# A graph attention layer on one core: eight gather buffers instead of four, and all 98 table scatters behind the last gather

## The chip, the core and the metric

The kernel runs on one core of a Trainium2 chip. The metric is the device time of one execution in microseconds (us). The core has five engines that matter here: TensorE (PE), VectorE (DVE), ScalarE (ACT), GpSimd (POOL) and SyncE (SP). Each runs its own list of instructions in order, and they wait for one another through semaphores. Direct DMAs are issued by SP; indirect DMAs, which take row numbers from memory, by POOL.

## What is computed

The reference is one layer of a graph network, on 50,000 nodes with 256 features and 12,500 edges plus one self loop a node. Cut to what matters:

```python
h = relu(layernorm(x))
xs, xd = (h @ W_src.T), (h @ W_dst.T)            # 8 heads of 32
alpha = sum(xs[src] * a_s[etype]) + sum(xd[dst] * a_d[etype])   # per head, loops included
alpha = leaky_relu(alpha, 0.2)
a = exp(alpha - segment_max(alpha, dst)[dst])
a = a / segment_sum(a, dst)[dst] * edge_weight
out = segment_sum(xs[src] * a, dst) + bias
h1 = layernorm(out + h, ln1)
ff = gelu(h1 @ W1.T + b1) @ W2.T + b2
result = x + layernorm(h1 + ff, ln2)
```

## The kernel before

The edges come sorted by destination. They are cut into NCH = 98 chunks of 128, handled as NPAIR = 49 pairs of chunks. The program has three stages and a piece between the first and the second.

**Edge stage** (up to some 404 us). For each pair POOL gathers four tiles of 128 rows of x (two chunks, source and destination rows) into a buffer of `xb` with four indirect DMAs (L653). DVE takes their statistics (L377, L381, and L398 to L409 once for two pairs), ACT writes the normalised and rectified rows to `h` (L417), PE transposes them (L426), ACT and DVE split the result into a high and a low part (L435, L442), and PE projects the four tiles with 24 matmuls (L459) into `ps_x` and `ps_f` or `ps_a`. ACT copies out the scores (L807, L808, and L810 after the fourth tile), and DVE then makes the messages (L1002), which SP stores. Step j of ACT's loop takes the `h` of pair j + 3 and the scores of pair j; step j of DVE's takes the statistics of pair j + 5 and the message of pair j - 1. A buffer of `xb` is free again when the `h` of its pair is written. So the gather of pair j waits on `h_ready` for pair j - XB, here j - 4.

**Between**: PE, DVE and ACT compute the softmax over each node's edges (about 404 to 446 us).

**Sum stage** (446 to 555 us). For each pair DVE weighs the loaded messages (L1223), PE adds up the edges of each node with a matrix of ones and zeros (L1442 transposes a line of destinations, ACT makes the matrix in L838 and L841, L1453 multiplies), DVE makes the record (L1230), and SP stores it in `sums`.

**Node stage** (the rest). All nodes in 98 groups of 512: POOL gathers each node's record from `sums` (L696) and the feed-forward matmuls (L1470, L1485 to L1487) follow.

To find a node's record, POOL scatters the place of each record into one of four tables in memory (`row_of`, L663), one indirect DMA of 128 entries a chunk, 98 in all. The function is `place`. Each scatter waits for the one four before it, which wrote the same table. After all of them the tables are read back (L687) and joined by DVE (L1378), and only then can the node stage gather.

POOL's order is written out by hand. 15 of the scatters stand between the gathers, one behind every third pair (`PLACE_AT`), and 83 behind the last gather. Three times among the 83 POOL also computes the reciprocal root for the first three groups of nodes (`input_rstd`, L669 and L671), ahead of scatters number 23, 33 and 73 counted from 0 (`RSTD_AT`). Each time it waits for DVE's statistics of that group (L1009 to L1017). DVE takes those of group 0 near the end of the edge stage, of group 1 right behind it, and of group 2 at step 12 of the sum stage (`STATS2_AT`).

Of the kernel before, what the change touches and what calls it, by code (L numbers as in the profile page):

```python
# [28 lines left out]
F32 = mybir.dt.float32  # L29
# [3 lines left out]
ACT = mybir.ActivationFunctionType  # L33
# [56 lines left out]
XB = 4  # L90
# [9 lines left out]
PLACE_AT = range(4, 49, 3)  # L100
RSTD_AT = (len(PLACE_AT) + 8, len(PLACE_AT) + 18, len(PLACE_AT) + 58)
# [16 lines left out]
def build(nc, x, ends_cols, next_cols, type_cols, weight_cols, dst_line, w_src_t, w_dst_t,  # L118
# [19 lines left out]
    assert D == KC * P and NODES < NR <= NROWS and NCH % 2 == 0 and NCH < P and EP % BLOCKS == 0 and NPAIR > max(RELU2_AT, PLACE_AT[-1]) and NCH > RSTD_AT[2] and D == 2 * P and QS * KC * SQ == D  # L138
# [18 lines left out]
    with ExitStack() as ctx:  # L157
# [19 lines left out]
        zt = [sb(f"zt_{n}", [P, 2, KC, GR], F32R) for n in ("hi", "lo")]  # L177
        act_hi = sb("act_hi", [P, AB, GR], F32R)
        act_lo = sb("act_lo", [P, AB, GR], F32R)

        xb = sb("xb", [P, XB, TG, D])
# [150 lines left out]

        def wide(a, dims):

            return a.to_broadcast(dims)
# [37 lines left out]
        def front_stats(eng, f):  # L373

            wait_count(eng, x_stats, TG * f.n)
            for t in range(TG):
                eng.bn_stats(stat[:, t, :], xb[:, f.off % XB, t, :]).then_inc(stat_step, 1)  # L377
            eng.wait_ge(stat_step, TG * f.n + TG)
            eng.sem_inc(dve_gate, 1)
            for t in range(TG):  # L380
                eng.bn_aggr(mv[:, f.off % 4, t, :], stat[:, t, :]).then_inc(x_stats, 1)  # L381
# [30 lines left out]
        def front_relu(eng, f):  # L412

            eng.wait_ge(x_scaled, f.n // 2 + 1)
            wait_count(eng, xt_turned, KC * (f.n - 1))
            for t in range(TG):
                eng.activation(h[:, f.par, t, :], xb[:, f.off % XB, t, :], ACT.Relu,  # L417
                               bias=shift[:, f.off % 4, t:t + 1], scale=rstd[:, f.off % 4, t:t + 1]).then_inc(h_ready, 1)
# [178 lines left out]
        def _(pool):  # L597
# [48 lines left out]
            def gather(j):  # L646
# [3 lines left out]
                for t in range(TG):  # L650
                    wait_count(pool, h_ready, TG * (j.n - XB) + t + 1)
                    at = edge_ends[:, 2 * j.n + t % 2, 1 - t // 2:2 - t // 2]
                    pool.indirect_dma_start(xb[:, b, t, :], None, x,  # L653
# [19 lines left out]
            def pair(j):  # L673
                gather(j)
                if j.n == PLACE_AT[0]:
                    pool.wait_ge(target_ready, 1)
                    pool.wait_ge(rows_cleared, 16 * RB)
                if j.n in PLACE_AT:
                    place(Step(0, PLACE_AT.index(j.n), NCH))
            pool.wait_ge(in_order, 1)  # L680
            steps(pool, pair, 0, NPAIR, *PAIR_LOOP)
            steps(pool, place, len(PLACE_AT), NCH, NCH, NCH, RB)
# [919 lines left out]
```

## Time and profile before

| | us |
|---|---|
| median of three runs | 3073.79 |
| the three runs | 3061.24, 3073.79, 3077.57 |
| span of the profiled execution | 3075.7 |
| busy in it: PE, DVE, POOL, ACT | 2838.8, 2303.7, 2211.0, 1798.2 |
| mean granted share of TensorE's clock | 0.959 |

The profiled execution is a single one. Its span, from the first to the last instruction, is the time that the sums below are made against; the table has no other time of it. The three runs differ by 16 us among themselves. Most of the time is the node stage, where PE is the busiest engine. The change touches the first 555 us.

### The profile page before, as it was taken

The numbers are of one execution on the slowest core, as the hardware profiler recorded it, in microseconds if no ns is written. First come the engines' busy times: TensorE is split into PE (matmuls) and PEld (weight loads), VectorE is DVE, ScalarE is ACT, GpSimd is POOL, SyncE is SP. The second block draws the span as 40 slices with busy tenths as digits, with TensorE's granted clock in tenths as the row PEclk, the third lists the DMA queues.
The fourth block names the chain that finished last, engine by engine and source line by source line (L and its number), as shares of the span: only waits on it lengthen the run. The fifth ranks groups of instructions, "written<-read, shape, count | busy, mean of one in ns | idle before, by whom it ended". The sixth has DMA issues, their size and how long they took to land.

```text
span 3075.7 us, 55240 instructions
## 1 busy us (share of the span) xinstructions
PE 2838.8 (92%) x18391; PEld 2581.0 (84%) x18391; DVE 2303.7 (75%) x6041; ACT 1798.2 (58%) x3180; POOL 2211.0 (72%) x1689
## 2 busy tenths in 40 slices
PE   4777747699999999999999999999999999999998
PEld 3666635589999999999999999999999999999998
DVE  5665576577777777777777777777777777777776
ACT  3555435356666666666666666666666666666664
POOL 5655555577777777777777777777777777777773
PEclk9788778899999999999999999999999999999999
DMA  6444356455555555555555555555555555555551
GB/s 150 99 112 106 89 137 212 125 129 148 145 149 149 149 147 145 144 145 144 145 149 146 144 146 147 147 144 145 144 145 145 146 146 148 147 146 146 146 138 62
DMA packets 596928, 430.65 MB, mean 140 GB/s; under 512 B 430521, under 2 KB 533471, under 8 KB 596644
## 3 DMA queue, kind: packets, MB, share of 16 engines
q1 hardware_dynamic: 563908, 348.13, 38.8%
q0 software_dynamic: 31616, 77.93, 13.7%
q8 instruction: 148, 2.42, 0.3%
q14 instruction: 136, 1.11, 0.1%
q10 hardware_dynamic: 1120, 1.05, 0.1%
HBM read 247.76 MB, written 179.26 MB: 139 GB/s over the span
## 4 chain that ended last, share of the span: by engine, by line
PE 80%; POOL 1%; DMA 0%; DVE 0%; ACT 0%; issue 0%; SPq 0%; DVEq 0%; POOLq 0%; ACTq 0%
PE ps_f L1470 35%; PE ps_x L1509 9%; PE ps_t L1485 6%; PE ps_t L1487 6%; PE ps_a L1485 6%; PE ps_a L1487 6%; PE ps_t L1486 6%; PE ps_a L1486 6%; POOL arena L696 0%; ACT arena L867 0%; DMA arena<-z_rows 0%; POOL arena L714 0%; DMA z_rows<-arena 0%; DMA arena<-sums,node_rows 0%; POOL zt_lo L734 0%
## 5 line engine op out<-in xcount | busy, mean ns | idle before, releaser
L847 ACT ACTIVATE act_hi<-ps_f,hidden_bias 128x512 fp32r<-128x512 f32 x784 | 538.2, 686 | 923.8 <-PE ps_f L1470 923.3
L1330 DVE TENSOR_TENSOR act_lo<-ps_f,act_hi 128x512 fp32r<-128x512 f32 x784 | 539.9, 689 | 468.5 <-ACT ps_f L848 401.7
L1470 PE MATMUL ps_f<-zt_hi,ffn_hi 128*128 128x512 f32 x1568 | 618.8, 395 | 7.2 <-DVE act_lo L1330 5.6
L1470 PE MATMUL ps_f<-zt_hi,ffn_lo 128*128 128x512 f32 x1568 | 620.2, 396 | 0.0
L1470 PE MATMUL ps_f<-zt_lo,ffn_hi 128*128 128x512 f32 x1568 | 618.0, 394 | 0.0
L848 ACT ACTIVATE ps_f<-ps_f,hidden_bias 128x512 f32<-128x512 f32 x784 | 511.0, 652 | 0.0
L696 POOL DMA_INDIRECT arena<-sums,node_rows x391 | 404.5, 1034 | 111.9 <-issue 92.6
L1485 PE MATMUL ps_a<-ffn_hi,act_hi 128*128 128x256 f32 x1568 | 439.8, 280 | 0.0
L1487 PE MATMUL ps_a<-ffn_hi,act_lo 128*128 128x256 f32 x1568 | 439.1, 280 | 0.0
L1485 PE MATMUL ps_t<-ffn_hi,act_hi 128*128 128x256 f32 x1560 | 438.1, 281 | 0.0
L1486 PE MATMUL ps_a<-ffn_lo,act_hi 128*128 128x256 f32 x1568 | 437.9, 279 | 0.0
L1487 PE MATMUL ps_t<-ffn_hi,act_lo 128*128 128x256 f32 x1560 | 437.4, 280 | 0.0
L1486 PE MATMUL ps_t<-ffn_lo,act_hi 128*128 128x256 f32 x1560 | 436.2, 280 | 0.0
L1470 PEld LDWEIGHTS ps_f<-zt_hi,ffn_lo 128*128 128x128 f32 x1568 | 293.9, 187 | 71.6
L1470 PEld LDWEIGHTS ps_f<-zt_hi,ffn_hi 128*128 128x128 f32 x1568 | 294.5, 188 | 44.4 <-DVE act_lo L1330 6.2
L1470 PEld LDWEIGHTS ps_f<-zt_lo,ffn_hi 128*128 128x128 f32 x1568 | 294.6, 188 | 36.1
L1485 PEld LDWEIGHTS ps_a<-ffn_hi,act_hi 128*128 128x128 f32 x1568 | 294.1, 188 | 18.1
L1486 PEld LDWEIGHTS ps_a<-ffn_lo,act_hi 128*128 128x128 f32 x1568 | 293.8, 187 | 18.4
L1486 PEld LDWEIGHTS ps_t<-ffn_lo,act_hi 128*128 128x128 f32 x1560 | 293.1, 188 | 18.2
L1485 PEld LDWEIGHTS ps_t<-ffn_hi,act_hi 128*128 128x128 f32 x1560 | 293.0, 188 | 18.1 <-issue 0.2
L1487 PEld LDWEIGHTS ps_a<-ffn_hi,act_lo 128*128 128x128 f32 x1568 | 295.2, 188 | 0.0
L1487 PEld LDWEIGHTS ps_t<-ffn_hi,act_lo 128*128 128x128 f32 x1560 | 294.2, 189 | 0.0
(243 smaller groups left out, 6665.2 us busy)
## 6 DMA issues: line engine op xcount, KB each, us to landing
xb<-in_x SPq DMA_DIRECT2D x97, 512.0 KB, 5.0
z_rows<-arena SPq DMA_DIRECT2D x97, 512.0 KB
arena<-z_rows SPq DMA_DIRECT2D x388, 128.0 KB
out<-arena SPq DMA_DIRECT2D x97, 512.0 KB, 4.3
h_rows<-h SPq DMA_DIRECT2D x96, 512.0 KB
arena<-h_rows SPq DMA_DIRECT2D x384, 128.0 KB
msgs<-arena SPq DMA_DIRECT2D x49, 256.0 KB
arena<-msgs SPq DMA_DIRECT2D x49, 256.0 KB, 6.9
```

The lines of the kernel that those rows point to most:

```text
L696: pool.indirect_dma_start(rec[:, g.par, t, :], None, sums, bass.IndirectOffsetOnAxis(ap=at, axis=0)).then_inc(rec_in[g.par], 16)
L847: act.activation(act_hi[:, m % AB, :], ps_f[:, m % 2, :], ACT.Gelu, bias=hidden_bias[:, m:m + 1]).then_inc(act_hi_ready, 1)
L848: act.activation(ps_f[:, m % 2, :], ps_f[:, m % 2, :], ACT.Gelu, bias=hidden_bias[:, m:m + 1]).then_inc(act_f_ready, 1)
L1330: dve.tensor_tensor(act_lo[:, m % AB, :], ps_f[:, m % 2, :], act_hi[:, m % AB, :].bitcast(F32), ALU.subtract).then_inc(act_lo_ready, 1)
L1470: ins = pe.matmul(ps_f[:, m % 2, 0:cols], ffn1[a][:, k, m * P:(m + 1) * P], zt[b][:, i.par, k, 0:cols], start=(j == 0), stop=(j == 3 * KC ...
L1485: pe.matmul(to, act_hi[:, m % AB, cols], ffn2[0][:, m, :], start=(m == 0 and t % 2 == 0), stop=False, skip_group_check=True)
L1486: pe.matmul(to, act_hi[:, m % AB, cols], ffn2[1][:, m, :], start=False, stop=False, skip_group_check=True)
L1487: ins = pe.matmul(to, act_lo[:, m % AB, cols], ffn2[0][:, m, :], start=False, stop=(m == MF - 1), skip_group_check=True)
L1509: ins = pe.matmul(to, xt[b][:, k, t * P:(t + 1) * P], lift[c][:, k, :], start=(j == 0 and t % 2 == 0), stop=(j == 3 * KC - 1), skip_group_ ...
```

## The change

The gathers go round eight buffers instead of four. Buffers 0 to 3 are the tensor `xb` as before. Buffers 4 to 7, `xb_early`, lie in the memory of `act_hi` and `act_lo`, which are written first in the node stage. The gather of pair j waits for the `h` of pair j - 8. No scatter stands between the gathers any more: all 98 come behind the last one. The three `input_rstd` stand ahead of scatters 14, 26 and 78. Nothing is changed in what the other engines do or in their order; they only read other buffers.

```diff
-XB = 4
+XB = 8
+XK = 4
-PLACE_AT = range(4, 49, 3)
-RSTD_AT = (len(PLACE_AT) + 8, len(PLACE_AT) + 18, len(PLACE_AT) + 58)
+RSTD_AT = (14, 26, 78)
...
+        with nc.sbuf_tensor("xb_early", [P, XB - XK, TG, D], F32) as xb_early:
+            pass
         act_hi = sb("act_hi", [P, AB, GR], F32R)
         act_lo = sb("act_lo", [P, AB, GR], F32R)
...
-        xb = sb("xb", [P, XB, TG, D])
+        xb = sb("xb", [P, XK, TG, D])
...
+        def gather_buf(f):
+
+            b = f.off % XB
+            return xb[:, b, :, :] if b < XK else xb_early[:, b - XK, :, :]
...
-                    pool.indirect_dma_start(xb[:, b, t, :], None, x,
+                    pool.indirect_dma_start(gather_buf(j)[:, t, :], None, x,
...
             def pair(j):
                 gather(j)
-                if j.n == PLACE_AT[0]:
-                    pool.wait_ge(target_ready, 1)
-                    pool.wait_ge(rows_cleared, 16 * RB)
-                if j.n in PLACE_AT:
-                    place(Step(0, PLACE_AT.index(j.n), NCH))
             pool.wait_ge(in_order, 1)
             steps(pool, pair, 0, NPAIR, *PAIR_LOOP)
-            steps(pool, place, len(PLACE_AT), NCH, NCH, NCH, RB)
+            pool.wait_ge(target_ready, 1)
+            pool.wait_ge(rows_cleared, 16 * RB)
+            steps(pool, place, 0, NCH, NCH, NCH, RB)
```

POOL's instructions at the start of the edge stage, before. L653 is a gather, L663 a scatter.

```order
L643 MEMSET arena 128x1
L653 DMA xb<-in_x,arena 128x256 x20
L663 DMA row_of<-arena 50304x1
L653 DMA xb<-in_x,arena 128x256 x12
L663 DMA row_of<-arena 50304x1
```

The same place in the changed kernel, where L661 is the gather.

```order
L651 MEMSET arena 128x1
L661 DMA xb<-in_x,arena 128x256 x16
L661 DMA xb_early<-in_x,arena 128x256 x16
L661 DMA xb<-in_x,arena 128x256 x16
L661 DMA xb_early<-in_x,arena 128x256 x16
```

The scatters behind pair 4 and every third pair after it are gone from here, and every other four pairs go to `xb_early`.

POOL from the last gathers to the reading back of the tables, before. L669 and L671 are `input_rstd`, L687 reads the tables.

```order
L653 DMA xb<-in_x,arena 128x256 x8
L663 DMA row_of<-arena 50304x1 x8
L669 TENSOR_TENSOR n_rstd<-n_var,minus_half 128x4
L671 TENSOR_TENSOR n_shift<-n_mm,n_rstd 128x4
L663 DMA row_of<-arena 50304x1 x10
L669 TENSOR_TENSOR n_rstd<-n_var,minus_half 128x4
L671 TENSOR_TENSOR n_shift<-n_mm,n_rstd 128x4
L663 DMA row_of<-arena 50304x1 x40
L669 TENSOR_TENSOR n_rstd<-n_var,minus_half 128x4
L671 TENSOR_TENSOR n_shift<-n_mm,n_rstd 128x4
L663 DMA row_of<-arena 50304x1 x25
L687 DMA node_rows<-row_of 128x391
```

The same in the changed kernel, where the lines are L661, L671, L677, L679 and L692.

```order
L661 DMA xb<-in_x,arena 128x256 x4
L671 DMA row_of<-arena 50304x1 x14
L677 TENSOR_TENSOR n_rstd<-n_var,minus_half 128x4
L679 TENSOR_TENSOR n_shift<-n_mm,n_rstd 128x4
L671 DMA row_of<-arena 50304x1 x12
L677 TENSOR_TENSOR n_rstd<-n_var,minus_half 128x4
L679 TENSOR_TENSOR n_shift<-n_mm,n_rstd 128x4
L671 DMA row_of<-arena 50304x1 x52
L677 TENSOR_TENSOR n_rstd<-n_var,minus_half 128x4
L679 TENSOR_TENSOR n_shift<-n_mm,n_rstd 128x4
L671 DMA row_of<-arena 50304x1 x20
L692 DMA node_rows<-row_of 128x391
```

Runs of 8, 10, 40 and 25 scatters have become runs of 14, 12, 52 and 20.

## Rows read from the trace of the kernel before

**Rows 1.** The page: its first line.

```profile
span 3075.7 us, 55240 instructions
```

**Rows 2.** Busy us by stage: length, PE, PEld, DVE, ACT, POOL, clock, DMA share, GB/s.

```profile
60.00:360.00 300.00, 222.20 (x1290) 205.31 (x1290) 191.53 (x678) 163.16 (x393) 173.84 (x177) 0.80 0.44 108
360.00:404.00 44.00, 31.70 (x211) 29.71 (x211) 24.96 (x87) 20.57 (x52) 11.33 (x13) 0.81 0.30 95
...
446.00:555.00 109.00, 75.78 (x331) 57.77 (x330) 69.52 (x114) 58.79 (x155) 55.86 (x56) 0.85 0.63 191
555.00:3076.00 2521.00, 2483.67 (x16420) 2264.88 (x16420) 1953.73 (x4972) 1530.25 (x2535) 1907.35 (x1365) 0.99 0.54 142
```

**Rows 3.** The gathers' line: ns min/median/max, first and last start, then idle before them.

```profile
L653 POOL DMA_INDIRECT xb<-in_x,arena x196: 943/949/5408, 9.8 to 359.3; - x196
...
  ACT h L417: 95.8, 56
  issue: 43.1, 139
```

**Rows 4.** The scatters, in the view of the tables.

```profile
L663 POOL DMA_INDIRECT row_of<-arena x98: 956/965/1992, 35.4 to 536.7; - x98
```

**Rows 5.** DVE's longest wait from 60 to 355 us: total, times, longest.

```profile
DVE arena L1002 <- ACT arena L810: 89.3, 20, 6.7
```

**Rows 6.** Timeline of the edge stage: start, us, engine, line, operation, [idle before <-releaser].

```profile
287.83 0.94 POOL L653 DMA_INDIRECT xb<-in_x,arena  x1 [0.30 <-issue]
...
290.56 0.19 ACT L810 COPY arena<-ps_a 128x32 f32<-128x32 f32 x1 [5.04 <-PE ps_f L459]
...
298.04 1.40 DVE L377 BATCH_NORM_STATS2 stat<-xb 128x6 f32<-128x256 f32 x4
...
300.94 0.29 PE L459 MATMUL ps_a<-proj_hi,zt_lo 128*128 128x272 f32 x1
...
302.54 1.01 POOL L663 DMA_INDIRECT row_of<-arena  x1 [0.31 <-issue]
...
305.42 0.19 ACT L810 COPY arena<-ps_a 128x32 f32<-128x32 f32 x1 [5.07 <-remote]
...
307.37 0.97 POOL L653 DMA_INDIRECT xb<-in_x,arena  x1 [3.82 <-ACT h L417]
...
318.87 0.19 ACT L810 COPY arena<-ps_a 128x32 f32<-128x32 f32 x1 [3.67 <-PE ps_x L459]
```

**Rows 7.** Timeline: POOL's first long pause, before the gather of pair 6.

```profile
47.66 0.95 POOL L653 DMA_INDIRECT xb<-in_x,arena  x1 [6.20 <-ACT h L417]
```

**Rows 8.** Timeline of ACT and POOL at the end of the edge stage.

```profile
354.60 2.10 ACT L417 ACTIVATE h<-xb,shift,rstd 128x256 f32<-128x256 f32 x4
...
371.16 0.97 POOL L663 DMA_INDIRECT row_of<-arena  x1 [1.25 <-DMA row_of<-arena]
...
373.75 2.08 ACT L417 ACTIVATE h<-xb,shift,rstd 128x256 f32<-128x256 f32 x4
...
399.58 1.06 POOL L669 TENSOR_TENSOR n_rstd<-n_var,minus_half 128x4 f32<-128x4 f32 x1 [27.45 <-DVE n_mm L1017]
...
401.95 0.19 ACT L810 COPY arena<-ps_f 128x32 f32<-128x32 f32 x1 [0.79 <-PE ps_f L459]
```

**Rows 9.** Timeline of the sum stage, all engines.

```profile
449.26 0.69 DVE L1230 TENSOR_TENSOR arena<-ps_a,rows 128x512 f32<-128x512 f32 x1 [1.63 <-PE ps_a L1453]
...
465.60 1.03 PE L1453 MATMUL ps_a<-arena 128*128 128x256 f32 x4
...
477.62 0.96 POOL L663 DMA_INDIRECT row_of<-arena  x1 [0.30 <-issue]
...
478.90 0.69 DVE L1230 TENSOR_TENSOR arena<-ps_a,rows 128x512 f32<-128x512 f32 x1 [13.79 <-remote]
...
495.96 1.41 POOL L669 TENSOR_TENSOR n_rstd<-n_var,minus_half 128x4 f32<-128x4 f32 x1 [17.38 <-DVE n_mm L1017]
...
554.05 0.69 DVE L1230 TENSOR_TENSOR arena<-ps_a,rows 128x512 f32<-128x512 f32 x1 [0.17 <-PE ps_a L1453]
```

More of the change, by code:

```diff
@@ L137, in build @@
     NQ = GR // SQ
-    assert D == KC * P and NODES < NR <= NROWS and NCH % 2 == 0 and NCH < P and EP % BLOCKS == 0 and NPAIR > max(RELU2_AT, PLACE_AT[-1]) and NCH > RSTD_AT[2] and D == 2 * P and QS * KC * SQ == D
+    assert NB == XK and (XB - XK) * TG * D == 2 * AB * GR and (NPAIR - NB) % XB > XK and NPAIR % XB == 1
+    assert D == KC * P and NODES < NR <= NROWS and NCH % 2 == 0 and NCH < P and EP % BLOCKS == 0 and NPAIR > RELU2_AT and NCH > RSTD_AT[2] and D == 2 * P and QS * KC * SQ == D
     sums = nc.dram_tensor("sums", (EP + P, D), F32, kind="Internal").ap()
@@ L376, in front_stats @@
             for t in range(TG):
-                eng.bn_stats(stat[:, t, :], xb[:, f.off % XB, t, :]).then_inc(stat_step, 1)
+                eng.bn_stats(stat[:, t, :], gather_buf(f)[:, t, :]).then_inc(stat_step, 1)
             eng.wait_ge(stat_step, TG * f.n + TG)
@@ L416, in front_relu @@
             for t in range(TG):
-                eng.activation(h[:, f.par, t, :], xb[:, f.off % XB, t, :], ACT.Relu,
+                eng.activation(h[:, f.par, t, :], gather_buf(f)[:, t, :], ACT.Relu,
                                bias=shift[:, f.off % 4, t:t + 1], scale=rstd[:, f.off % 4, t:t + 1]).then_inc(h_ready, 1)
```

## The prediction

> **What bounds the kernel now.** I read the busy times by stage first, then the waits inside each stage. The node stage is 2521 us of the 3075.7, with PE busy 98.5% of it [rows 1, 2]. The change touches nothing there, so the sum concerns the first 555 us: how early the node stage can begin. It begins when two things are done, DVE's last record at 554.05 + 0.69 us [rows 9] and the scatters with the reading back of their tables. The last scatter starts at 536.7 [rows 4]. That is 17 us before DVE is through, and the landing and the reading back lie between, so DVE's records end last, but the scatters have no more than those few microseconds to spare.
>
> In the edge stage no engine is full: from 60 to 360 us PE is busy 74%, DVE 64%, POOL 58%, at a granted clock of 0.80 [rows 2], between the levels of 1.2 and 2.4 GHz. POOL sits idle 95.8 us until ACT has written an `h` [rows 3]. That looks like a shortage of buffers. But the reader should see in [rows 6] when the data of one pair is wanted. The last gather of pair 38 is issued by 288.77, and DVE comes to its statistics at 298.04, straight from its earlier work, with no idle time before them. The data is not what DVE waits for. DVE waits for ACT's L810 before L1002, 89.3 us in 20 waits [rows 5], and L810 waits for PE.
>
> That last wait is the odd one. The last matmul of pair 33 starts at 300.94 and takes 0.29 us, yet ACT's copy of its result starts at 305.42, after 5.07 us of idleness [rows 6]. So PE's signal comes about 4.2 us after its matmul. What happens at 305.42? POOL's run of indirect DMAs ended at 303.55. The same is seen at 290.56, where the run had ended at 288.77: 1.8 us after the run in both. Then `h` is written, POOL starts its next two gathers of four DMAs, and the cycle begins again. The sum stage shows the same thing more clearly: PE's L1453 starts at 465.60 and DVE's record of it at 478.90, after 13.79 us idle, 0.3 us after POOL's last scatter of a long run ended at 478.58 [rows 9]. I take as the working rule that PE's increments arrive late while POOL issues indirect DMAs back to back, and arrive when POOL pauses. Why that is so, no row tells.
>
> **The scatters taken out of the edge stage.** The cycle of two pairs that holds a scatter lasts 305.42 - 290.56 = 14.86 us, the next one, without, 318.87 - 305.42 = 13.45 [rows 6]. A scatter lengthens POOL's run and with it the cycle by 1.4 us. Thirteen of the 15 stand before the gather of pair 44: 13 x 1.4 = 18 us gained by the time that the `h` of pair 40 is written. That one stands two cycles before the 354.60 of pair 44 [rows 8], at 354.6 - 14.9 - 14.9 = about 325.
>
> **Four more buffers, in the steady state.** POOL issues a gather as soon as an `h` frees a buffer, with four buffers and with eight. It is always the faster one: a gather takes 0.95 + 0.31 us [rows 3], a pair 5.0 us against cycles of 6.7 us a pair. The cycle stays at 13.45 and I cost this part at nothing. What hides the gathers is the 9 us by which they lead; it becomes some 36 us.
>
> **Four more buffers, at the start.** Before, POOL issues six pairs and then pauses 6.2 us until 47.66 [rows 7]. Now ten pairs are free to go: four pairs x 5.0 = 20 us more of unbroken run, to about 60 us. If PE's increments wait for its end, the start loses 60 + 2 - 45 = 17 us. If they leak through as fast as in the cycles, it loses nothing. No row shows so long a run of gathers; I take the middle, 9 us, and keep 0 and 18.
>
> **The end of the edge stage.** The `h` of pair 40 is then written at 325 - 18 + 9 = 316, and the last gather, pair 48's, is issued by 322, where before it ended at 360.3. Now come 14 scatters instead of 8. The eight took from 360.3 to 372.1 [rows 3, 8], 1.5 us each, and in that time the edge stage stood almost still: no `h` between 354.60 and 373.75 [rows 8]. Fourteen take 21 us, to 343, and I expect the `h` of pair 42 at 345. Behind it ACT has ten steps. From 373.75 to 401.95 it made seven, 4.0 us each [rows 8], with POOL quiet. Five of the ten carry DVE's statistics as well, which add 1.2 us: 5 x 5.2 + 5 x 4.0 = 46. The stage ends at 391 instead of 402, **11 us earlier**, 2 to 20 by the bounds of the start.
>
> **The sum stage.** POOL then has 12 + 52 scatters to the third `input_rstd`, where it had 10 + 40. The 50 took from 399.58 to 478.58 [rows 8, 9]. The 14 more cost 1.27 us each, 18 us, so POOL gets there at 478.6 - 11 + 18 = 486. Against that stands DVE: it must reach step 12. Before, it made five records from 449.26 up to POOL's pause at 478.9, 5.9 us each, and the remaining six in the 17 us behind, 2.8 us each [rows 9]. Now its first record is at 438 and 48 us go by until the pause: eight records, and four steps are left, 11 us. The third `input_rstd` is then at 497, against 495.96. The wait there shrinks from 17.4 us to 11.
> Behind it stood 25 scatters, about 1.6 us each to 536.7 [rows 4, 9]; now 20, over by 530. The records that follow step 12 took from 496 to 554.7 and keep their pace; five fewer scatters beside them may give 1.5 us. So the sum is +1 - 1.5, and the likely end of DVE's records lies between 552 and 556. The gain of the edge stage is given back, since the scatters cost about the same beside the sum stage.
>
> **The sum.** 3075.7 - 11 (edge stage) + 12 (longer way from there to step 12) - 1.5 (fewer scatters behind it) gives 3075. POOL's idle time before the first `input_rstd`, 27.45 us [rows 8], grows to about 45, and PE runs freely in it; for what the 5.2 us a pair may be too high there I take off 2 us, an estimate without a row: 3073. The bounds of the start, 9 us either way, shift it all. The median of the runs stood 1.9 us below the span, so the prediction is **3071 us**, 3061 to 3081 for this likeliest case.
>
> **Rival A: the buffers were the bound.** The Trainium skill, Perfetto Trace Analysis, section Optimization Strategy, says that the same gap repeating on an engine that should be saturated can mean too few buffers. POOL's 3.8 us before every other pair [rows 6] is such a gap. As a mechanism of this kernel: POOL would run on at 5.0 us a pair and the rest follow at the 5.2 us a pair used above. From pair 2's `h`, at about 47 [rows 7], 47 more pairs take 245 us, so that the edge stage ends near 300 and some 90 to 100 us go: 2975 to 2985, or about 3025 if half of it comes. Against it stands the 9 us that a pair's data lies unused. I give 0.08. By that rule the kernel gains 3%; by [rows 6] nothing comes of the buffers.
>
> **Rival B: slower.** PE's increments stay away for as long as POOL does not pause. The start then loses 18 us, the run of 52 scatters lets DVE make six records only, and six steps at 2.8 us are left at the pause: the third `input_rstd` comes at 478.6 - 2 + 18 + 17 = 512, and the records end at 512 + 59 = 571, 16 us late: **3090**. It decides from the point at which fewer than seven records stand before the pause. For it speaks the 13.79 us wait [rows 9], against it that five records did get through earlier. The same section of the skill's Perfetto Trace Analysis advises to interleave stages with different busiest engines, which this change undoes; that would come out on this side. I give 0.15 to slower by over 0.5%.
>
> **Rival C: faster by more.** The start loses nothing, so that the edge stage ends 20 us earlier, and DVE makes its records at 4 us each beside the scatters, so that it is at step 12 when POOL gets there, at 478.6 - 20 + 18 = 477 instead of 496. The records then end some 19 us earlier: 3050 to 3058. I give 0.19.
>
> **How the numbers follow.** The likeliest case has 0.58, A 0.08, B 0.15, C 0.19. A difference under 0.5%, 15 us, is about what a measurement cannot tell from none. Faster by over that is A and most of C, with a little of the likeliest's edge: 0.26; slower is B: 0.14; the same 0.60. The range leaves out A and the far ends of B: 3042 to 3090.
>
> **What the profile would show.** No scatter row before the last gather, which ends near 322 (315 to 332); POOL's first long pause at 60 or later; 13.4 to 13.5 us from one long wait of L810 to the next; POOL idle 40 us or more before the first `input_rstd`, at about 389; the third near 497, after a wait shorter than 17 us; the last record at 550 to 558. Wrong it would be if the cycle gets clearly shorter than 13.45 us, if DVE is seen waiting for a gather, if PE's signals come in time during POOL's long runs, or if the node stage, 2521 us, changes in length.

## The result, and the profile after

The changed kernel takes 3077.12 us, the kernel before 3061.64, medians of 20 executions each, taken side by side (3064.95 to 3087.50 without one execution of 3602.31 at a granted clock of 0.742, and 3051.36 to 3077.57). The ratio is 1.0044, 95% interval 1.0029 to 1.0059. So the change costs 0.44%, 13.5 us, where I forecast about 3 us less than the 3073.79 that stood for the kernel before. The new time lies inside my range; the direction is wrong.

One thing comes first. The profile that the prediction was read from has a span of 3075.7 us [rows 1], and its execution took 3077.57: of the 20 executions of that kernel it is the slowest. The profile after is from an execution of 3070.53 us, one of the shorter ones. Held against each other these two say that the change gains 7 us. A later profile of the kernel before (run e16) has a span of 3057.7, from an execution of 3059.41 us, near the 3061.64 of this comparison, and is the better partner. But it comes from a chip on which the kernel before takes 3075 us in the median, and it was the fastest of its ten there. Both profiles are used below, and a second one of the changed kernel (e15, 3076.17 us) beside them.

The page of the kernel after, its first line, and then the busy time by stage (length, PE, PEld, DVE, ACT, POOL, clock, DMA share, GB/s), which answers to [rows 2]:

```profile
span 3068.8 us, 55240 instructions
```

```profile
60.00:360.00 300.00, 216.28 (x1376) 204.04 (x1375) 198.25 (x703) 169.58 (x409) 167.42 (x171) 0.86 0.35 107
...
446.00:555.00 109.00, 68.86 (x306) 51.49 (x306) 67.15 (x111) 53.27 (x142) 57.25 (x57) 0.86 0.67 197
555.00:3068.00 2513.00, 2482.76 (x16418) 2266.62 (x16418) 1952.94 (x4967) 1531.81 (x2535) 1908.91 (x1365) 0.99 0.54 142
```

PE's busy time in the node stage is 2482.76 us against 2483.67 in [rows 2]. As forecast, all that happens lies ahead of it. The timeline of the kernel after shows the places (start, us, engine, line, operation, then the idle time and its releaser). First the start and the end of the edge stage:

```profile
57.38 2.08 ACT L425 ACTIVATE h<-xb,shift,rstd 128x256 f32<-128x256 f32 x4 [2.91 <-remote]
72.58 2.08 ACT L425 ACTIVATE h<-xb,shift,rstd 128x256 f32<-128x256 f32 x4
...
73.45 0.95 POOL L661 DMA_INDIRECT xb<-in_x,arena  x1 [7.94 <-ACT h L425]
...
329.80 1.02 POOL L671 DMA_INDIRECT row_of<-arena  x1 [0.30 <-issue]
...
345.77 0.97 POOL L671 DMA_INDIRECT row_of<-arena  x1 [3.44 <-DMA row_of<-arena]
...
383.53 1.06 POOL L677 TENSOR_TENSOR n_rstd<-n_var,minus_half 128x4 f32<-128x4 f32 x1 [25.44 <-DVE n_mm L1022]
...
385.90 0.19 ACT L815 COPY arena<-ps_f 128x32 f32<-128x32 f32 x1 [0.79 <-PE ps_f L467]
```

POOL's first pause comes at 73.45 instead of 47.66 [rows 7], and the edge stage ends at 385.90 instead of 401.95 [rows 8]. Then the way to the first record and the sum stage:

```profile
411.55 2.08 ACT L827 ACTIVATE h<-xb,n_shift,n_rstd 128x256 f32<-128x256 f32 x4 [19.32 <-POOL n_shift L679]
...
441.65 0.69 DVE L1235 TENSOR_TENSOR arena<-ps_a,rows 128x512 f32<-128x512 f32 x1 [1.63 <-PE ps_a L1458]
...
497.18 1.04 POOL L677 TENSOR_TENSOR n_rstd<-n_var,minus_half 128x4 f32<-128x4 f32 x1
...
498.53 2.08 ACT L827 ACTIVATE h<-xb,n_shift,n_rstd 128x256 f32<-128x256 f32 x4 [11.55 <-POOL n_shift L679]
...
503.83 0.69 DVE L1235 TENSOR_TENSOR arena<-ps_a,rows 128x512 f32<-128x512 f32 x1 [12.97 <-PE ps_a L1458]
...
546.06 0.69 DVE L1235 TENSOR_TENSOR arena<-ps_a,rows 128x512 f32<-128x512 f32 x1 [0.50 <-PE ps_a L1458]
```

The same places in the better profile of the kernel before, e16:

```profile
54.78 2.08 ACT L417 ACTIVATE h<-xb,shift,rstd 128x256 f32<-128x256 f32 x4
...
398.58 1.06 POOL L669 TENSOR_TENSOR n_rstd<-n_var,minus_half 128x4 f32<-128x4 f32 x1 [18.17 <-DVE n_mm L1017]
400.95 0.19 ACT L810 COPY arena<-ps_f 128x32 f32<-128x32 f32 x1 [0.79 <-PE ps_f L459]
...
417.68 2.07 ACT L822 ACTIVATE h<-xb,n_shift,n_rstd 128x256 f32<-128x256 f32 x4 [10.80 <-POOL n_shift L671]
...
448.28 0.69 DVE L1230 TENSOR_TENSOR arena<-ps_a,rows 128x512 f32<-128x512 f32 x1 [1.63 <-PE ps_a L1453]
...
484.21 1.33 POOL L669 TENSOR_TENSOR n_rstd<-n_var,minus_half 128x4 f32<-128x4 f32 x1
...
495.21 2.06 ACT L822 ACTIVATE h<-xb,n_shift,n_rstd 128x256 f32<-128x256 f32 x4
...
536.54 0.69 DVE L1230 TENSOR_TENSOR arena<-ps_a,rows 128x512 f32<-128x512 f32 x1 [0.64 <-PE ps_a L1453]
```

Read the changed kernel's rows against those of e16. Its edge stage ends 15.1 us earlier. The first record comes only 6.6 us earlier: ACT, which makes the exp behind its second `input_relu`, waits 19.32 us for POOL's second `input_rstd` instead of 10.80. The last record comes 9.5 us later: between the first and the last lie 104.4 us instead of 88.3. And of the 16 us between these, 13 are one wait that e16 does not have. ACT comes to its third `input_relu`, in step 26 of the sum stage, and POOL has not made the third `input_rstd`; PE then waits for ACT, 12.0 us, and DVE for PE, 12.97. In e16 POOL had begun it 11 us before ACT came. The spans differ by 11.1 us, the medians by 15.5.

The profile of e15 repeats this: the edge stage ends at 387.81, ACT waits 23.36 us ahead of the exp and 14.16 for the third `input_rstd`, which POOL begins at 506.81 without a wait of its own, and DVE then waits 15.38 us; the last record starts at 552.93.

### The profile page after: what moved, and what is told of

It is laid out like the page before. It is cut to its first block, busy times and chain, and to the rows that moved or that the text cites. A ratio compares the mean times of both kernels' runs of the same rounds, so it can differ in the third digit from the quotient of the medians.

```text
span 3068.8 us, 55240 instructions
## 1 busy us (share of the span) xinstructions
PE 2815.0 (92%) x18391; PEld 2565.3 (84%) x18391; DVE 2304.9 (75%) x6041; ACT 1799.2 (59%) x3180; POOL 2211.3 (72%) x1689
## 4 chain that ended last, share of the span: by engine, by line
PE 80%; POOL 1%; DMA 0%; DVE 0%; ACT 0%; issue 0%; SPq 0%; DVEq 0%; POOLq 0%; ACTq 0%
PE ps_f L1475 35%; PE ps_x L1514 9%; PE ps_t L1492 6%; PE ps_t L1491 6%; PE ps_a L1492 6%; PE ps_t L1490 6%; PE ps_a L1491 6%; PE ps_a L1490 6%; DMA arena<-z_rows 0%; POOL arena L701 0%; ACT arena L872 0%; POOL arena L719 0%; DMA arena<-sums,node_rows 0%; DMA z_rows<-arena 0%; POOL zt_lo L739 0%
## 5 line engine op out<-in xcount | busy, mean ns | idle before, releaser
L1475 PEld LDWEIGHTS ps_f<-zt_lo,ffn_hi 128*128 128x128 f32 x1568 | 295.5, 188 | 33.5
```

Of the source, the lines that this page charges most:

```text
L1475: ins = pe.matmul(ps_f[:, m % 2, 0:cols], ffn1[a][:, k, m * P:(m + 1) * P], zt[b][:, i.par, k, 0:cols], start=(j == 0), stop=(j == 3 * KC ...
```

## The experiments

The runs fell on five chips, and they are of two kinds. On three of them the kernel before takes 2965 us (runs e1 to e12), on the two others 3062 and 3075 (e13 to e15, and e16 to e18). The comparison above is of the second kind. I call them the 2965 chips and the 3062 chips. A ratio always compares kernels on the same chip; two ratios that stand side by side can be from two chips of one kind (e1 to e4, e5 to e8 and e9 to e12 each had one chip).

**e1: the kernel before again.** No edit.

> The kernel before, unchanged, for a second profile and for what two timings of one kernel differ by. The profile that the prediction rests on has a span of 3075.7 us, the longest of 20 executions, whose median is 3061.6. Theory L (the sum started from an unlucky execution): the second profile is some 10 to 15 us shorter, and the difference lies in the sum stage and the stalls of PE and DVE there, so that its last record ends near 540 instead of 554. Theory N (the node stage differs from execution to execution): the last record ends near 554 again and the node stage is shorter than 2521 us by 10 or more. The ratio should be 1.000, within 0.002.

2964.22 against 2965.27 us, ratio 1.0000, 0.9991 to 1.0009. It told nothing of L and N, as it was another kind of chip: the edge stage ends at 308.35 instead of 401.95. The waits of e1 from 60 to 355 us (engine and line, what they waited for: total, times, longest) show why:

```profile
POOL xb L653 <- ACT h L417: 20.8, 50, 4.8
DVE stat L377 <- DMA xb<-in_x,arena: 12.2, 8, 3.3
...
DVE arena L1002 <- ACT arena L810: 7.2, 6, 2.1
```

The wait of [rows 5], 89.3 us, is 7.2 here. POOL issues just as many DMAs back to back, but PE's increments are not late. The last matmul of one tile in e1 ends at 199.68, and ACT copies its result at 199.72, in the middle of a run of POOL's:

```profile
199.39 0.29 PE L459 MATMUL ps_a<-proj_hi,zt_lo 128*128 128x272 f32 x1
...
199.72 0.20 ACT L810 COPY arena<-ps_a 128x32 f32<-128x32 f32 x1
```

POOL's idle time before a gather that an `h` releases is 0.4 us on average, hardly more than the 0.3 us before any other, so its own issuing is the pace: on the 2965 chips I read the edge stage as bound by POOL. With the scatters out of it (e3) it ends 13.1 us earlier, at 295.22, which fits.

**e2 and e8: the buffers alone.**

```diff
-RSTD_AT = (14, 26, 78)
+PLACE_AT = range(4, 49, 3)
+RSTD_AT = (len(PLACE_AT) + 8, len(PLACE_AT) + 18, len(PLACE_AT) + 58)
```

> The change's first part alone: eight gather buffers, and the 15 scatters between the gathers as before. Theory S (the start is what costs): POOL's first run has ten or more pairs, the relu of pair 3 comes near 72 instead of 50.6, the edge stage stays some 16 us behind, and the time is 3071 to 3080, ratio 1.003 to 1.006. Theory T (the scatters beside the sum stage are what costs): the start is caught up before the edge stage ends, and the time is 3058 to 3066, ratio 0.999 to 1.001.

> The kernel of e2 again, eight buffers with the scatters in their old places, beside the others. Both theories: a ratio of 0.997 to 0.999 if these executions have an edge stage of about 300 us as in e1; where the edge stage takes some 390 us, as in the two profiles shown first, the longer first run of gathers costs it up to 17 us at the start and the ratio is 1.000 to 1.005.

0.9977 (0.9968 to 0.9986) and 0.9980 (0.9971 to 0.9989): a gain, which neither theory had. The edge stage ends 2.7 us earlier in e2 than in e1, and DVE's waits for gathers fall from 12.2 us to 4.6 + 3.6, as its waits from 60 to 355 us say:

```profile
DVE stat L386 <- DMA xb<-in_x,arena: 4.6, 3, 2.1
DVE stat L386 <- DMA xb_early<-in_x,arena: 3.6, 3, 2.8
```

Where the gathers only just keep up, four more buffers seem to hide some late landings. The first gather of node records comes 2.8 us earlier than in e1, at 448.65; the spans differ by 5.4, and the rest was not followed.

**e3: the scatters alone,** with four buffers.

```diff
-PLACE_AT = range(4, 49, 3)
-RSTD_AT = (len(PLACE_AT) + 8, len(PLACE_AT) + 18, len(PLACE_AT) + 58)
+RSTD_AT = (14, 26, 78)
...
-                if j.n in PLACE_AT:
-                    place(Step(0, PLACE_AT.index(j.n), NCH))
...
-            steps(pool, place, len(PLACE_AT), NCH, NCH, NCH, RB)
+            steps(pool, place, 0, NCH, NCH, NCH, RB)
```

> The change's second part alone: four gather buffers as before, and all 98 scatters behind the last gather. Theory S: the edge stage gains the 18 us of the thirteen scatters, the longer row of scatters costs about as much behind it, and the time is 3055 to 3066, ratio 0.998 to 1.001. Theory T: the scatters beside the sum stage hold back the third input_rstd and the records by 10 to 20 us more than the edge stage gains, and the time is 3071 to 3080, ratio 1.003 to 1.006.

1.0039, 1.0025 to 1.0053, as T has it: on this kind of chip the whole loss is the scatters'.

**e4: the start held.**

```diff
-                    wait_count(pool, h_ready, TG * (j.n - XB) + t + 1)
+                    wait_count(pool, h_ready, TG * (j.n - (XK if j.n < 12 else XB)) + t + 1)
```

> The changed kernel, but the gathers of pairs 4 to 11 wait for the h of the pair four before, as with four buffers; from pair 12 on all eight are used. Theory S: the relu of pair 3 is back near 50, the burst comes later, at pairs 12 to 15, when PE is busy, and costs less than 17 us there; the time is 8 to 15 us below the changed kernel's, 3062 to 3069. Theory T: the start is of no weight, since POOL has the same scatters to make behind it; the time stays at 3074 to 3080.

1.0036, 1.0023 to 1.0050: nothing gained. e2 and e3, on the same chip, add up to 1.0016, so holding the start is if anything dearer. There is no late start to mend here: the `h` of pair 3 comes at 39.66 in e4, and at 40.27 in e5, where the first run of gathers is long. On the 2965 chips that run is of no weight, and Theory S fails.

**e5 and e15: the changed kernel again,** on either kind.

> The changed kernel, unchanged, for a second profile beside a second one of the kernel before. Both theories expect a ratio near that measured before, 1.003 to 1.006. Theory R (ACT waits for POOL's second and third input_rstd, which now stand behind 26 and 76 scatters in a row instead of 18 and 58): the profile has an ACT wait of 20 us or more for the second, ahead of the exp, and the first record comes 8 us or more later, against the end of the edge stage, than in the kernel before. Theory Q (the last scatter ends late, and the reading back with it): the reading back of the tables starts 10 us or more later than in the kernel before on the same chip, and behind DVE's last record or right beside it.

> The changed kernel a third time, for what the first comparison (1.0044) and e5 (1.0016) differ by. If the kernel before is at about 2965 us in these executions, both theories expect 1.001 to 1.003. If it is at about 3060, as in the first comparison, Theory S (the long first run of gathers delays PE's signals at the start, and the edge stage is bounded by them) expects 1.003 to 1.006 with the relu of pair 3 later by 15 us or more than in the kernel before.

e5: 1.0016, 1.0007 to 1.0025, smaller than expected, and close to the sum of the parts (-0.0023 of e2, +0.0039 of e3). e15: 1.0036, 1.0010 to 1.0061, with the relu of pair 3 at 73.06. In e5 both signs are seen, that of R in the first row, that of Q in the second. (The reading back is a direct DMA that POOL itself issues, so it stands behind all of POOL's scatters.) The rows below those are e1's:

```profile
334.09 2.07 ACT L827 ACTIVATE h<-xb,n_shift,n_rstd 128x256 f32<-128x256 f32 x4 [34.74 <-POOL n_shift L679]
...
449.94 0.60 POOL L692 DMA_DIRECT2D node_rows<-row_of  x1 [6.48 <-DMA row_of<-arena]
```

```profile
324.49 2.07 ACT L822 ACTIVATE h<-xb,n_shift,n_rstd 128x256 f32<-128x256 f32 x4 [10.21 <-POOL n_shift L671]
...
433.51 0.69 DVE L1230 TENSOR_TENSOR arena<-ps_a,rows 128x512 f32<-128x512 f32 x1 [0.50 <-PE ps_a L1453]
435.19 0.59 POOL L687 DMA_DIRECT2D node_rows<-row_of  x1 [4.71 <-DMA row_of<-arena]
```

**e6: the `input_rstd` early.**

```diff
-RSTD_AT = (14, 26, 78)
+RSTD_AT = (8, 18, 58)
```

> The changed kernel with its three input_rstd at scatters 8, 18 and 58 instead of 14, 26 and 78: as many scatters stand between the last gather and each of them as in the kernel before, and the 15 others behind the third. Theory R: ACT's wait ahead of the exp goes back to about 10 us, the records come 10 to 15 us earlier, and the ratio falls from 1.004 to 0.998 to 1.001. Theory Q: the exp and the first records come earlier as well, but the last scatter ends where it did, so the gather of the node records moves by less than 5 us; the ratio stays at 1.002 to 1.004.

1.0014, 1.0005 to 1.0023: nothing gained against e5, as Q has it. The cause that R names was there and is gone, but something else ends last. In the rows of e6 the last record is 24 us earlier than in e5, at 429.65, and the tables are read back at 450.17 as before; DVE stands idle for them, 24.86 us:

```profile
429.65 0.69 DVE L1235 TENSOR_TENSOR arena<-ps_a,rows 128x512 f32<-128x512 f32 x1 [0.51 <-PE ps_a L1458]
...
450.17 0.60 POOL L692 DMA_DIRECT2D node_rows<-row_of  x1 [4.51 <-DMA row_of<-arena]
...
455.20 1.77 DVE L1383 TENSOR_TENSOR node_rows<-node_rows,arena 128x391 int32<-128x391 int32 x3 [24.86 <-DMA arena<-row_of]
```

**e7: buffers alone, with the second `input_rstd` two scatters behind the first.**

```diff
-RSTD_AT = (len(PLACE_AT) + 8, len(PLACE_AT) + 18, len(PLACE_AT) + 58)
+RSTD_AT = (len(PLACE_AT) + 8, len(PLACE_AT) + 10, len(PLACE_AT) + 58)
```

> Eight gather buffers, 15 scatters between the gathers as before, and the second input_rstd only two scatters behind the first, instead of ten. Theory R: the exp comes as soon as DVE's statistics allow, some 8 to 10 us earlier, and the records with it, if the scatters are not the limit; the ratio is 0.994 to 0.997. Theory Q: the scatters end where they did with eight buffers alone, and the ratio stays at 0.997 to 0.999.

0.9992, 0.9983 to 1.0001, against 0.9980 of e8 on the same chip: if anything slower, where R expected a gain. ACT's wait ahead of the exp is gone, and in its place the exp waits 10.80 us for DVE's L1204. The first record starts 47.4 us behind the end of the edge stage, in e8 47.3. So on this kind of chip the 10 us that ACT waits in the kernel before cost nothing, and only what comes on top of them does.

**e9: eight tables, four read back.** The rows that the four others hold are left out of the result.

```diff
-RB = 4
+RB = 8
+RR = 4
...
-            dve.wait_ge(node_rows_in, 16 * RB)
-            for i in range(RB - 1):
+            dve.wait_ge(node_rows_in, 16 * RR)
+            for i in range(RR - 1):
```

> The changed kernel with eight scatter tables in place of four, so that a scatter waits for the landing of the eighth one before it; only four of the tables are read back, so the rows that the four others hold are left out of the result. In e5 the 98 scatters took 182 us from the last gather on, 1.86 us each against 1.27 where one follows another without a wait. Theory Q (in a row the scatters are paced by their landings): the row shrinks to 130 to 145 us, the third input_rstd comes 20 us or more earlier, and the ratio falls to 0.990 to 0.997. Theory P (POOL's queue is the limit whatever the table): the row stays at 170 us or more and the ratio at 1.000 to 1.003.

0.9932, 0.9918 to 0.9945: Q. The row of scatters takes 148.1 us instead of 181.8, a little more than the 130 to 145 expected, and the third `input_rstd` comes at 382.39 instead of 415.69. The view of the tables (with the idle time before them), first of e5, then of e9:

```profile
L671 POOL DMA_INDIRECT row_of<-arena x98: 953/962/2002, 261.6 to 442.4; - x98
...
  DMA row_of<-arena: 62.1, 38
  issue: 23.6, 61
```

```profile
L672 POOL DMA_INDIRECT row_of<-arena x98: 954/958/2004, 261.2 to 408.3; - x98
...
  issue: 26.5, 84
  DMA row_of<-arena: 16.9, 15
```

A scatter between gathers shows the 0.3 us of any DMA before it and no wait for a landing, as its table's last scatter is several pairs old. In a row 38 of the 98 wait for the landing of the fourth before them: 62.1 us in all, 33.5 in e1.

**e10: half of the scatters moved.**

```diff
-PLACE_AT = range(4, 49, 3)
-RSTD_AT = (len(PLACE_AT) + 8, len(PLACE_AT) + 18, len(PLACE_AT) + 58)
+PLACE_AT = range(4, 49, 6)
+RSTD_AT = (len(PLACE_AT) + 11, len(PLACE_AT) + 22, len(PLACE_AT) + 68)
```

> Eight gather buffers, and 8 of the 15 scatters between the gathers (behind every sixth pair) instead of all or none; the input_rstd stand in proportion, at 11, 22 and 68 scatters behind the last gather. Theory Q: the cost grows with each scatter that is moved, so the ratio lies between those of e8 (0.998) and e5 (1.0016), at 0.999 to 1.001. Theory B (two ends balance: the records end earlier and the scatters later, and the later of the two counts): the first few moved scatters cost nothing or gain, ratio 0.996 to 0.998.

0.9981, 0.9971 to 0.9991: as B has it, not Q. Seven moved scatters cost nothing against e8 (0.9980, another chip of this kind), all fifteen 0.36% (e5). The reading back starts at 432.72 and the last record ends at 434.28; the two are still level.

**e11: fifteen scatters not made,** their rows left out of the result; the edit is against e6.

```diff
-            steps(pool, place, 0, NCH, NCH, NCH, RB)
+            steps(pool, place, 0, NCH - 15, NCH - 15, NCH - 15, RB)
```

> The changed kernel with the input_rstd of e6 (8, 18, 58) and the last 15 scatters not made at all; the rows that they would write are left out of the result. Against e6 it prices fifteen scatters at the end of the row. Theory Q: the reading back starts 20 to 28 us earlier than in e6 (15 x 1.3 to 1.86), before DVE's last record, which then is what ends last, and the ratio is 0.993 to 0.997. Theory R (the scatters' end is of no weight): the ratio stays at 1.0014.

0.9956, 0.9943 to 0.9970, against 1.0014 of e6: Q. The reading back starts at 429.50 instead of 450.17, 20.7 us earlier, 1.4 us for each scatter left out. The last record ends at 428.19, so the two are about level, and neither is last by much.

**e12: no wait of POOL's before the first `input_rstd`.**

```diff
-RSTD_AT = (len(PLACE_AT) + 8, len(PLACE_AT) + 18, len(PLACE_AT) + 58)
+RSTD_AT = (len(PLACE_AT) + 13, len(PLACE_AT) + 20, len(PLACE_AT) + 62)
```

> Eight buffers with 15 scatters between the gathers, and the input_rstd at 13, 20 and 62 scatters behind the last gather instead of 8, 18 and 58. In e8 POOL waits 8.7 us for DVE before the first; here five more scatters fill that time. Theory Q: the reading back of the tables starts some 8 us earlier, at about 425, and the records, which end at 431, become the last; the ratio falls from 0.998 to 0.996 to 0.997. Theory R: ACT's second wait grows by 2 to 3 us, the exp and the records come later by as much, and the ratio is 0.998 to 1.000.

0.9978, 0.9968 to 0.9987, the same as e8; its interval takes in the top of Q's range. The reading back starts at 431.70 and not at 425, because it waits for DVE's last record, as its row says; so the records are what ends last, as Q has it:

```profile
431.70 0.59 POOL L696 DMA_DIRECT2D node_rows<-row_of  x1 [4.32 <-DVE arena L1239]
```

The last scatter starts only 1.4 us earlier than in e8 (426.43 and 427.81). Where the rest of the 8.7 us went wasn't followed up.

**e13: eight tables, all read back.** `other_rows` moves to the memory of the early gather buffers.

```diff
-RB = 4
+RB = 8
...
-        other_rows = prob[:, 6:2 * HEADS, :].rearrange("p h e -> p (h e)")[:, 0:(RB - 1) * NT].bitcast(I32).rearrange("p (b t) -> p b t", b=RB - 1)
+        other_rows = xb_early.rearrange("p b t d -> p (b t d)")[:, 0:(RB - 1) * NT].bitcast(I32).rearrange("p (b t) -> p b t", b=RB - 1)
```

> The changed kernel with eight scatter tables, all eight read back and merged (into the memory of the four early gather buffers, which are free by then), so that nothing is left out. Against e9 it has four more reads, of 0.54 us each on POOL's queue while DVE is still at its records, and four more merges of 0.56 us behind the last record. Theory Q: the row of 98 scatters takes about 148 us as in e9, the merges cost 2 us, and the ratio is 0.993 to 0.996. Theory P2 (what e9 gained came from what it left out): the ratio is over 0.998.

This run fell on a 3062 chip and turned everything round: 1.0100, 1.0066 to 1.0135, where the changed kernel has 1.0036 on the same chip (e15). It can't be compared with e9, and says nothing on Q against P2. But see the first records of e13, and POOL from 440 to 480 us:

```profile
446.70 0.69 DVE L1235 TENSOR_TENSOR arena<-ps_a,rows 128x512 f32<-128x512 f32 x1 [6.91 <-remote]
...
462.14 0.69 DVE L1235 TENSOR_TENSOR arena<-ps_a,rows 128x512 f32<-128x512 f32 x1 [14.15 <-remote]
...
485.99 0.69 DVE L1235 TENSOR_TENSOR arena<-ps_a,rows 128x512 f32<-128x512 f32 x1 [22.56 <-remote]
```

```profile
L671 POOL DMA_INDIRECT row_of<-arena x32 | 30.7, 959 | 9.8 <-issue 9.5 <-DMA row_of<-arena 0.3
```

POOL's queue runs with hardly a wait for landings (0.3 us), and DVE makes two records in these 40 us. In the changed kernel, with four tables, the same 40 us hold 7.0 us of such waits, and 20 records:

```profile
L671 POOL DMA_INDIRECT row_of<-arena x24 | 26.0, 1082 | 15.0 <-issue 8.0 <-DMA row_of<-arena 7.0
```

That is the working rule of the prediction at full strength: on these chips PE's increments seem to get through in POOL's pauses. The other profiles of this kind fall in with it. From 440 to 480 us the scatters of e15 wait 12.8 us for landings and DVE makes 17 records, in e16 6.9 us and 15; in the profile of the kernel before it is 2.5 us and 6 records, in e18, which has four tables too, 1.7 us and 3. So the number of tables is not all that decides.

**e14: eight tables, with the scatters in their old places.**

> Eight gather buffers and eight tables, all read back, and the 15 scatters between the gathers in their old places. It differs from e13 in the place of the scatters and of the input_rstd alone. Theory Q: the scatters between the gathers do not wait for landings anyway and lengthen the edge stage by 1.3 us each, the records end at about 431 as in e8 and are last, so the ratio is 0.997 to 0.999 and e13 is faster than this one by 0.2 to 0.4%: with eight tables the move of the scatters is a gain. Theory P2: the order of e8 and e5 holds, this one is the faster of the two by 0.2% or more.

1.0076, 1.0043 to 1.0108, lower than e13 by 0.0024. That is the side of P2, but the two intervals overlap: not settled. e13 is slower than the changed kernel on the same chip (1.0036, 1.0010 to 1.0061); for e14 the intervals overlap.

**e16: the kernel before a third time.**

> The kernel before a third time, for a profile that is not from an unlucky execution. If it is at about 3060 us, Theory L (the profile of 3075.7 us had chance stalls in the sum stage) expects a span of 3052 to 3066, records that end at 535 to 545 instead of 554.7, and the edge stage's end still near 402; Theory N expects the records' end near 554 and a node stage shorter by 10 us. If it is at about 2965 us it repeats e1, and both expect a ratio of 1.000.

Ratio 0.9981, 0.9950 to 1.0012, span of the profile 3057.7. Its edge stage ends at 400.95, its records at 537.23: L. What [rows 9] show, 13.79 us of one wait and 17.38 of another, isn't in this execution. But it isn't a thing of one execution either: POOL waits for DVE before the third `input_rstd` 20.04 us in e18, 27.75 in e13 and 18.50 in e14, and not at all in e16, e17, e15 and the profile of the changed kernel. How often the kernel before has it, two profiles can't tell. And the same kernel against itself gave 0.9981 here, so a tenth or two of a per cent are within the noise on this chip.

**e17 and e18: buffers alone and scatters alone,** the kernels of e2 and e3 on a 3062 chip.

> Eight buffers alone. If the kernel before is at about 2965 us, 0.997 to 0.999 as in e2 and e8. If it is at about 3060, Theory S (PE's signals are late for the length of POOL's first run, which eight buffers lengthen) expects the relu of pair 3 at 70 or later instead of 50.6 and an edge stage that ends 5 to 17 us later: 1.003 to 1.006. Theory T (only the scatters cost) expects 0.999 to 1.001.

> Four gather buffers, all 98 scatters behind the last gather. If the kernel before is at about 2965 us, 1.003 to 1.005 as in e3. If it is at about 3060, Theory S expects the edge stage to gain 18 us or more and the ratio at 0.998 to 1.001; Theory T expects 1.003 to 1.006 here too, because ACT waits for the second and third input_rstd.

Buffers alone: 1.0047, 1.0017 to 1.0078. Scatters alone: 0.9996, 0.9964 to 1.0028. Both as S has it, and together they come to the 1.0044 of the change, though each interval is 0.3% wide to either side. The start of e17:

```profile
76.81 2.07 ACT L426 ACTIVATE h<-xb,shift,rstd 128x256 f32<-128x256 f32 x4
...
77.68 0.96 POOL L662 DMA_INDIRECT xb<-in_x,arena  x1 [8.29 <-ACT h L426]
```

The `h` of pair 3 is 22 us later than in e16, that of pair 12 14.6 us later (142.36 and 127.75), and the edge stage ends at 409.69, 8.7 later. In e18 the edge stage ends at 375.00, 26 us earlier, and the sum stage takes that back, with waits of DVE for PE as in e13:

```profile
459.37 0.69 DVE L1226 TENSOR_TENSOR arena<-ps_a,rows 128x512 f32<-128x512 f32 x1 [9.99 <-remote]
480.66 0.69 DVE L1226 TENSOR_TENSOR arena<-ps_a,rows 128x512 f32<-128x512 f32 x1 [20.00 <-remote]
```

No version that ran on both kinds of chip beats the kernel before on both. The buffers alone gain 0.2% on the one and lose 0.5% on the other.

## Why the prediction was wrong

**The base of the sum stage: the step that failed.** I put the third `input_rstd` at 497 "against 495.96". The 497 came true, 497.18. The 495.96 is the slow execution's; in e16 it is 484.21, and POOL does not wait there. So that execution has no 17.4 us of slack in front of it that a longer row of scatters could eat: each scatter more makes it later. Against e16 the terms of my sum measure: the edge stage -15.1 where I had -11; the longer way to the third `input_rstd` +28.0 where I had +12; what stands behind it -3.5 where I had -1.5. Together that is +9.5 us at the last record instead of about nothing, and +11.1 in the span.

That the 497 came true is luck. I had POOL there at 486 and waiting 11 us for DVE. POOL got there at 497.18 by its own work, with DVE's statistics long made, and it was ACT that had to wait. The later profile of the changed kernel (e15) has the same order, at 506.81. That an earlier `input_rstd` would take the loss back on these chips isn't shown: it was tried only on a 2965 chip (e6). What should have warned me: the median of the three executions lay 1.9 us below the span, but the lowest of them was 3061.24, 14 us below, and I took a wait of 13.79 us that occurs once for a property of every execution.

**The price of a scatter in a row: too low.** "The 14 more cost 1.27 us each." From the first to the third `input_rstd` the kernel after takes 113.7 us for 64 scatters, e16 85.6 for 50: 28.0 us for 14, 2.0 each. My own rows had 79 us for 50 of them, 1.58 each, so 1.27 was too low even by those. And the 14 behind the last gather take from 329.8 to 358.1, 2.0 each again, where I had 1.5. That the rest is the wait for the landing in one's own table is shown by e9, on a 2965 chip; here the rows say the same, with 37.0 us of such waits in the view of the tables against 26.9 in e16. I had the row of it, 1.25 us [rows 8], and didn't price it.

**The wait behind the second `input_rstd`: not seen.** I went from the end of the edge stage straight to the first record. The exp stands behind ACT's second `input_relu`, and that behind POOL's second `input_rstd`, which now comes after 26 scatters from the last gather on instead of 18. ACT's wait grows by 8.5 us, and of 15.1 us of the edge stage 6.6 are left.

**The start: right mechanism, too small.** I took 9 us between 0 and 18. The `h` of pair 3 is 17.8 us later than in e16: it waits for the end of the run, as Rival B had it. POOL's first run is also longer than the ten pairs that I counted: it goes on to 65.51 us, eleven pairs, as the `h` of pair 2, from 57.38 on, freed one more buffer in time. Two things don't fit the rule as I put it. ACT's second copy of pair 2's transposes, which PE had made by 61.54, starts at 72.09, 6.6 us after the run and not 1.8; why, no run tells. And it isn't PE's increments alone that are late. Each of DVE's steps to the reciprocal root needs the one before it. Within the run they come 1.4 us apart, as DVE waits for its own result:

```profile
52.49 0.17 DVE L411 SCALAR_TENSOR_TENSOR newton<-mv,rstd 128x8 f32<-128x8 f32 x1 [1.24 <-DVE rstd L408]
53.88 0.17 DVE L414 SCALAR_TENSOR_TENSOR rstd<-newton,root 128x8 f32<-128x8 f32 x1 [1.23 <-DVE newton L411]
```

In e5, on a 2965 chip and within the same run of gathers, the first of them shows no wait and they are 0.20 us apart:

```profile
35.89 0.17 DVE L411 SCALAR_TENSOR_TENSOR newton<-mv,rstd 128x8 f32<-128x8 f32 x1
```

All five profiles of eight gather buffers on the 3062 chips have this 1.2 us (also e13, e14, e15 and e17), and none of the fifteen others has it. Near 26 us, early in the run, the same steps are 0.20 us apart on these chips too, so the lateness isn't there from the run's start.

**The edge stage: right.** The cycle is 13.4 us, as said (gathers at 145.71, 159.19 and 172.54). The `h` of pair 40 came at 323.88 where I had 316, later by what the start was mis-sized, but the stage ended at 385.90, in e15 at 387.81, where I had 391. I had let it stand still during the 14 scatters; it went on beside them, with the `h` of pair 44 at 353.75, before the last of them. POOL's idle time before the first `input_rstd` is 25.44 us for the same reason, where I had 40 or more. (Fourteen scatters stand before the gather of pair 44, not thirteen; for the `h` of pair 40, which the sum uses, thirteen is right.)

**The buffers in the steady state: right on the chip that I looked at.** From the `h` of pair 12 to that of pair 40 e17 takes 202.8 us, the kernel before 201.4 and 206.0 (e16); without scatters between the gathers it is 187.5 with eight buffers and 188.7 with four (e18). Rival A is refuted there. The Trainium skill (Perfetto Trace Analysis, section Optimization Strategy) says that a repeating gap can mean too few buffers; for the 3.8 us of [rows 6] it did not. On the 2965 chips the buffers gain 0.2%, perhaps through DVE's waits for landings (e2), which this trace did not have. The advice of the same section to interleave stages with different busiest engines: e3, with its loss of 0.39% on a 2965 chip, agrees by its sign, but what grew there was the scatters' waits for landings (62.0 us against 33.5), and e18 shows no loss on a 3062 chip.

**Rival B** was the right one by its direction, at a smaller size than its 3090 or its 0.5%: the start's loss in full, the third `input_rstd` too late. Its mechanism in the sum stage, few records beside the scatters and POOL waiting for DVE, is that of e13 and e18. The two profiles of the changed kernel don't have it: there the records go on beside a row with more waits for landings, and the `input_rstd` is late by POOL's own row.

What stays open: what makes increments late on the 3062 chips and not on the others, and which executions on them fall into the long waits of [rows 9]. No run told that apart.

## What to carry to other kernels

Before a sum is made from one profile, hold its span against all the times of that kernel: if it is among the longest, look for waits that occur once, and don't spend them as slack. When work is moved to the end of an engine's queue, ask of every item behind it who waits for that, and price a row of DMAs that share a few targets by their landings and not by their issue; it had been cheap between the gathers because time passed there. A gain on one chip of this kind need not be one on another: the same edit gave 0.998 and 1.0047.

## What the hardware showed that I had not expected

The same program takes 2965 us on three chips and 3062 to 3075 on two, and it all lies ahead of the node stage: the edge stage ends at 308.35 in e1 and at 400.95 in e16, the first gather of node records starts at 451.46 and 548.68, and the spans are 2961.4 and 3057.7. DVE's L1002 waits 7.2 us for L810 on the one (e1), and on the other, from 60 to 355 us of e16:

```profile
DVE arena L1002 <- ACT arena L810: 81.0, 19, 6.6
```

With POOL's indirect DMAs issued back to back at 0.95 us each on both, the increments of PE, and in the long first run DVE's own, come late on one kind only. There, waits in POOL's queue seem worth having: with eight tables, which take most of them away (e13), the kernel has a ratio of 1.0100, against 1.0036 of the changed kernel on the same chip.
